# Windowed row maxima in blocks of 64 queries by 128 keys, on two column tiles of TensorE

## The reference

```python
# 1: attention with rotary positions, 16 heads of 16, over the last 64 keys
q, k = rotary(q), rotary(k)
attn = q @ k.T / 4
allowed = (j <= i) & (i - j < 64)
attn = softmax(where(allowed, attn, -inf)) @ v
x = layernorm(x + attn @ w_out.T)
# 2: a gated feed-forward with a shift by one token
x = layernorm(x + sigmoid(xr @ W_r.T) * (relu(xk @ W_k.T) ** 2 @ W_v.T))
# 3: linear attention with random features
x = layernorm(x + linear_attention(x, Wq, Wk, Wv, Wo, random_features))
# 4: a block with causal attention over all keys, and 8 experts of which each token takes 2
x = layernorm(x + block(x))
```

## Time and profile before

| | |
|---|---|
| median of 3 runs | 1870.25 us |
| the profiled execution's own time | 1865.49 us |
| its span, first to last instruction | 1863.7 us |
| TensorE, matmuls | 1708.6 us busy, 92% |
| TensorE, weight loads | 1100.9 us, 59% |
| VectorE | 1014.7 us, 54% |
| ScalarE | 887.6 us, 48% |
| GpSimd | 835.6 us, 45% |
| granted TensorE clock, mean | 0.959 |

### The profile page before, as it was taken

How to read it: one execution, slowest core, us unless ns; L and a number is a source line. 1 busy time by engine, 2 the same in 40 slices (tenths; PEclk the granted TensorE clock), 3 DMA queues, 4 the chain that set the end, 5 groups by cost and what they waited for, 6 DMA issues and landing times. The chain is left out here.

```text
span 1863.7 us, 32872 instructions
## 1 busy us (share of the span) xinstructions
PE 1708.6 (92%) x10796; PEld 1100.9 (59%) x10796; DVE 1014.7 (54%) x2357; ACT 887.6 (48%) x1877; POOL 835.6 (45%) x1295
## 2 busy tenths in 40 slices
PE   6888998999999999999999999999569999999992
PEld 4556766565567666556666654644337766667771
DVE  4547776877757786865788677886401100011014
ACT  2445454556665465675637467577322222212223
POOL 4664565432358683235858323446352211221123
PEclk9889998999999899999989999999779999999996
DMA  6655235042154404215432214050053133332126
GB/s 214 88 184 68 35 81 70 2 59 78 20 81 76 97 8 69 69 27 73 88 49 36 36 47 69 13 105 5 29 189 85 33 71 83 91 88 63 20 23 192
DMA packets 105668, 131.21 MB, mean 70 GB/s; under 512 B 15499, under 2 KB 77084, under 8 KB 105361
## 3 DMA queue, kind: packets, MB, share of 16 engines
q1 hardware_dynamic: 89104, 117.08, 29.3%
q0 software_dynamic: 14336, 11.41, 4.3%
q10 hardware_dynamic: 2064, 0.61, 0.2%
HBM read 53.96 MB, written 38.01 MB: 49 GB/s over the span
## 5 line engine op out<-in xcount | busy, mean ns | idle before, releaser
L1095 ACT ACTIVATE b_probs<-b_psum 128x512 f32<-128x512 f32 (+3 forms) x896 | 418.2, 547 | 190.3 <-PE b_psum L959 188.6
L1359 DVE TENSOR_REDUCE b_mneg<-b_psum 128x2 f32<-128x384 f32 (+5 forms) x608 | 333.2, 591 | 94.6 <-PE b_psum L946 92.4
L1458 POOL TENSOR_SCALAR_AFFINE_SELECT b_probs<-b_probs 128x512 f32<-128x512 f32 (+1 forms) x400 | 239.4, 610 | 292.9 <-ACT b_probs L1095 282.2
L946 PE MATMUL b_psum<-b_qk 96*128 96x192 bf16 (+4 forms) x1280 | 297.9, 299 | 4.2 <-DVE b_write_at L1319 1.2
L959 PE MATMUL b_psum<-b_qk 99*128 99x192 bf16 (+5 forms) x1344 | 262.9, 290 | 14.9 <-DMA b_qk<-b_mrow 11.2
L1689 POOL DMA_INDIRECT before_last_norm<-b_ye,b_ids x64 | 99.0, 1547 | 349.0 <-DMA before_last_norm<-b_ye,b_ids 191.5
L1784 ACT ACTIVATE b_hid<-b_psum,b_b 128x512 f32<-128x512 f32 (+1 forms) x136 | 90.0, 662 | 336.3 <-PE b_psum L1727 336.3
L1828 DVE TENSOR_TENSOR b_ye<-b_psum,b_b2b 128x512 f32<-128x512 f32 (+1 forms) x33 | 22.3, 675 | 388.9 <-PE b_psum L1735 388.9
L1735 PE MATMUL b_psum<-b_w,b_hid 128*128 128x256 f32 x1024 | 222.8, 379 | 0.6 <-ACT b_hid L1784 0.6
L1727 PE MATMUL b_psum<-b_xgt,b_w 128*128 128x512 f32 (+1 forms) x544 | 221.7, 567 | 0.0
L1735 PEld LDWEIGHTS b_psum<-b_w,b_hid 128*128 128x128 f32 x1024 | 193.9, 190 | 27.0 <-ACT b_hid L1784 1.0
(11 more groups left out here) (217 smaller groups left out, 2427.3 us busy)
## 6 DMA issues: line engine op xcount, KB each, us to landing
b_qk<-b_split SPq DMA_DIRECT2D x372, 128.0 KB, 5.1
b_w<-in_W SPq DMA_DIRECT2D x16, 1024.0 KB, 8.3
slot_rows<-before_last_norm SPq DMA_DIRECT2D x8, 1024.0 KB, 11.1
b_xg<-slot_rows SPq DMA_DIRECT2D x16, 512.0 KB, 9.6
before_last_norm<-b_early SPq DMA_DIRECT2D x4, 1024.0 KB, 4.9
b_o<-before_last_norm SPq DMA_DIRECT2D x4, 1024.0 KB, 5.7
before_last_norm<-b_o SPq DMA_DIRECT2D x4, 1024.0 KB, 4.4
b_rows<-before_last_norm SPq DMA_DIRECT2D x8, 512.0 KB, 7.4
```

What stands on the lines that cost most here:

```text
L946: ins = pe.matmul(out[:, i, :], q[0:KS, h, P * t:P * t + P], q[0:KS, HG + h, a:e], start=not last, stop=True, skip_group_check=True)
L1095: act.activation(probs_of((g, h2, t), a, e)[:, heads[0]:heads[-1] + 1, :], bank, ACT.Exp, scale=SCALE).then_inc(s.exp_done, 1)
L1359: dve.tensor_reduce(out, in_bank(("max",) + x[1:], heads, e - a), AX.X, ALU.max, negate=True).then_inc(s.max_read, 1)
L1458: ins = pool.affine_select(out=block, in_=block, pattern=[[0, HG], [1 if ahead else -1, z - y]], compare_op=ALU.is_ge, fill=none, base=y - ...
```

## The change

The windowed tile's keys are given as its own 128 (`key_spans`), and all its four heads go into one bank of 512 columns. Each tile of 128 queries is cut in two blocks of 64 queries. A block needs the 64 keys before it and its own 64, so 128 keys: the first block's scores go to partitions 0 to 63 of the bank, the second block's to partitions 64 to 127, each by a matmul with 64 stationary columns on its own half of the array (`tile_position`). One mask of 128 columns serves all tiles and is repeated for the four heads; a second one, for the first tile, hides the missing keys. A windowed group then has eight pieces, each with one mask matmul of 512 columns, eight score matmuls and one reduction of 512 columns.

`pieces` no longer asks whether a group is windowed. In the second pass, cells of 128 and of 64 queries therefore become one piece of four heads in place of two pieces of two. The estimated cost of `max` at L379 is not edited; it follows from the new numbers of heads and keys.

```diff
     def key_spans(self, g, t):
         if self.windowed[g]:
-            return [(max(0, P * t - WINDOW), P * t + P)]
+            return [(P * t, P * t + P)]
 ...
     def pieces(self, g, a, e):
-        n = 2 if self.windowed[g] else 4 if e - a <= P else 2 if e - a <= 2 * P else 1
+        n = 4 if e - a <= P else 2 if e - a <= 2 * P else 1
         return [(tuple(range(k, k + n)), a, e) for k in range(0, HG, n)]
 ...
                     if windowed[g]:
-                        pe.matmul(out, u.id16[:, :], u.mask_q[:, :, WQ - (e - a):WQ], start=True, stop=True,
-                                  skip_group_check=True)
-                    elif last:
+                        pe.matmul(out, u.id16[:, :], u.mask_q[:, int(t == 0), :].unsqueeze(1).broadcast_to([P, len(heads), P]),
+                                  start=True, stop=True, skip_group_check=True)
+                        for i, h in enumerate(heads):
+                            for y in range(2):
+                                at = P * t + WINDOW * y
+                                lo = max(0, at - WINDOW)
+                                ins = pe.matmul(out[WINDOW * y:WINDOW * y + WINDOW, i, lo - at + WINDOW:P],
+                                                q[0:KS, h, at:at + WINDOW], q[0:KS, HG + h, lo:at + WINDOW],
+                                                start=False, stop=True, tile_position=(0, WINDOW * y), skip_group_check=True)
+                        ins.then_inc(s.max_ready, 1)
+                        continue
+                    if last:
 ...
-    behind = p + WINDOW - w
-    mask_q = np.where((behind >= 0) & (behind < WINDOW), 0.0, NEG)
+    behind = p % WINDOW + WINDOW - f
+    near = (behind >= 0) & (behind < WINDOW)
+    mask_q, mask_first = np.where(near, 0.0, NEG), np.where(near & ((p >= WINDOW) | (f >= WINDOW)), 0.0, NEG)
 ...
-            [np.eye(P), mask_q, mask_q, np.where(f <= p, 0.0, NEG),
+            [np.eye(P), mask_q, mask_first, np.where(f <= p, 0.0, NEG),
 ...
-    sbuf(nc, ctx, u, "mask_q", [P, 2, WQ], BF16)
+    sbuf(nc, ctx, u, "mask_q", [P, 2, P], BF16)
 ...
-    width = [P, 2 * WQ, P, P]
+    width = [P, 2 * P, P, P]
```

More of the change, by code:

```diff
@@ L1502, in by_tile @@
         return np.tile(x.reshape(NT, P, HD).transpose(1, 0, 2), HG).astype(np.float32)
-    p, w, f = np.arange(P)[:, None], np.arange(WQ)[None], np.arange(P)[None]
-    behind = p + WINDOW - w
-    mask_q = np.where((behind >= 0) & (behind < WINDOW), 0.0, NEG)
+    p, f = np.arange(P)[:, None], np.arange(P)[None]
+    behind = p % WINDOW + WINDOW - f
+    near = (behind >= 0) & (behind < WINDOW)
+    mask_q, mask_first = np.where(near, 0.0, NEG), np.where(near & ((p >= WINDOW) | (f >= WINDOW)), 0.0, NEG)
     return {
```

## The result

The changed kernel takes 1877.28 us (median of six runs, 1874.61 to 1878.69); the kernel before, beside it, 1869.28 (1864.43 to 1870.53). The ratio is 1.005 with a 95% interval of 1.0037 to 1.0063: 8 us slower, where +5 was forecast and 1875 predicted. The profiled execution took 1877.8 us against 1865.5, so 12 us more, and what is read from the two traces concerns those 12. The size came out right. The experiments show that it is made of other terms than the sum had.

What follows compares the result with a forecast made beforehand. TensorE was taken to bound batches 1 to 3, batch 0 being latencies and loads. TensorE's tiles +6.4, relief -1.3 and batch 0 at 0 gave +5 us on the median of 1870.25: 1875 us, range 1860 to 1896.

Steps and rivals of the forecast that it cites:

- TensorE bounds batches 1 to 3: After 120 us TensorE, 96% busy, sets the pace; work added or removed there goes into the time one for one.
- the halved stream is given back: At seven of eight tiles, 0.22 us of streaming saved, 0.25 spent on two width changes and the exposed load.
- The sum of a tile: TensorE's cost of a windowed tile's maxima: 0.70 us, +0.04 at seven of eight tiles, +0.25 at tile 0.
- the weight load of a 64-column tile: Score matmuls: taken at the slow rate, 0.055 us, shown once ahead of the first pair; pairs at 0.058.
- rival B: Score matmuls: loads or streams of the two 64-column tiles don't overlap, +0.23 a tile, +22 us, 1897; chance 0.13.
- Relief of VectorE and ScalarE, -1.3: After 120 us: VectorE 49 us and ScalarE 9 us lighter; TensorE regains half of its 2.6 us of waits.
- Batch 0: Before 120 us, latencies and loads: between -5 and +3, taken as 0; the 8.4 us DMA wait isn't shortened.
- The order: Planner's static lists change with the maxima's estimated cost; idle time may move some 10 us either way; no term.
- rival C: The new order is bad, planned cost off by 0.26 a tile: 5 to 12 us of new waits, 1880 to 1887; chance 0.13.
- I expect none: TensorE's clock in the bursts: no fall expected, since streaming stays 0.44 of 0.70 us; no term.
- No drain (D): Width changes on TensorE cost nothing: 0.19 less a tile, -18 us on 96 tiles, 1857; chance 0.04.
- much relief (A): Lighter VectorE and ScalarE, fewer banks and batch 0 win more than the printed waits: -6 us, 1864; chance 0.20.

Runs made afterwards that it cites:

- e1: The changed kernel, order untouched, with the mask put in by two column-tiled matmuls of 64 stationary and 512 moving columns: 1854.87 us.
- e9 to e11: The changed kernel with the mask in column tiles too, planner told 0.55, 0.66 and 0.75 us for a windowed tile's maxima: 1856.3, 1848.88 and 1857.07 us.
- e4: The kernel before with only the second pass changed, cells of 128 and 64 queries as one piece of four heads: 1861.2 us.
- e3: The kernel before, work untouched, with the planner told 0.2195 us for each of a windowed tile's two pieces: 1859.76 us.

## Why the prediction was right, and what in it was not

- **TensorE bounds batches 1 to 3, and the halved stream is given back.** Right, and shown: the two changes of width are there with 0.095 us each, a tile costs 0.65 to 0.67 against 0.66, and taking 103 to 137 of some 550 changes away (e1, e9 to e11) brings 15.5 us at the same told cost, some of which may be the clock's.
- **The sum of a tile was 0.04 too high.** The mis-sized term is the weight load of a 64-column tile. I took the slow rate, 0.055 exposed and pairs 0.058 apart, 0.229 in all to the last pair's start behind the change of width; it was 0.19. So the load is nearer the fast end of my bounds. With 0.66 at every tile the term is 84 x 0 + 12 x (0.66 - 0.45) = +2.5 us in place of +6.4. (At tile 0 four of the eight matmuls have 64 columns, not one; their partners have 128, so the term stands. And the sixteen values matmuls would take 2.2 us one after another, not 2.1.)
- **Pairs overlap (rival B).** They do; B is out.
- **Relief of VectorE and ScalarE, -1.3.** The waits that I counted did not shrink together: those on maxima are gone in batch 1's burst and longer in batch 2's. TensorE's idle time in batch 1's stretch fell by 6 us, mostly in waits that I had not counted, by relief or by the list. The relief itself was 38 us of VectorE and 4 of ScalarE's exponentials, not 49 and 9: I multiplied mean durations, which overlap, where the busy time in the earlier trace rows has 111.5 + 12.7 = 124.2 us for the windowed reductions, and 108.4 - 21.9 = 86.5 is left of them. e4 leaves room for more, but can't be told from the list.
- **Batch 0, "nothing in the change shortens" the wait on the DMA, between -5 and +3.** The step that failed. The wait grew from 6.9 to 11.9 us, since the new list has SyncE issue six large DMAs while the rows come ready, and the instructions there came 13 us late. I read the wait in the earlier trace rows and did not look at what SyncE issued ahead of that DMA.
- **The order, "no term, but in the range", by some 10 either way.** The size was right, the place was not: it is the largest term of all. The reason I gave for rival C, that the planner is told too little, is not borne out as a rule: e3 is faster with the wrong cost. The changed work is fastest when told its true 0.66, but the mask in tiles, whose tile takes 0.46 in a run, is fastest at 0.66 as well. Rival C's mechanism, waits that weren't there, happened in part: the DMA, and two waits of 2.3 and 1.9 us on maxima in batch 2's burst.
- **"I expect none", a fall of the clock in the bursts.** Wrong for two of the three: 0.97 against 0.99 in batch 1's (120 to 300 us) and 0.96 against 0.99 in batch 2's (500 to 620), though 1.00 against 0.98 in batch 3's. With the 0.78 against 0.86 before 120 us the clock is a term that the sum put at nothing, and no run prices it by itself.
- **No drain (D), much relief (A).** D is out as said, and A too, since batch 1 was reached 13 us late and not 4 early. As forecast, the expert stage is unchanged: the 12.2 us at 1040 us are the 12.3 at the end. The forecast of 1875 against 1877 is luck in its sum: TensorE's term was 4 us too large, and the order, the DMA and the clock, left out or put at 0, can each be worth more than the 5 us of the whole sum.
- **The chances** gave slower 0.46, same 0.32 and faster 0.22. As measured, slower is right. For the work apart from its list, +4.9 with a standard error of 5.7, it is open which of the three is.

## What to carry to other kernels

Column tiles pay where a whole stretch of work stays at their width; a full-width matmul between tiled ones costs a change each way, here 0.095 us against some 0.2 that the tiles save. Put the mask into tiles too, and the same idea that lost brings 11 us over the work of before, from mean to mean and from best list to best list. And where a planner writes the order, run each version under three or four told costs before judging it: one list against one list here gave anything from -10 to +18 for the same edit. Behind a wait on a small DMA, look at when its data were ready, and at what its queue was given just before.

## What the runs showed of the hardware that I had not expected

- A 64-column bf16 tile loads faster than the float32 rate of the earlier trace rows: 0.055 us was expected to show ahead of the first pair. The 0.31 from mask to first pair leave nothing for it beside 0.22 and 0.095, and the three steps between pairs take 0.19 where their streams are 0.17, so 0.02 to 0.03 shows.
- Two matmuls with 64 stationary and 512 moving columns run side by side at full pace: 224.70 to 224.92, 0.22 us for both.
- A DMA of 12 rows behind six of 1 MB on one queue let TensorE wait 11.9 us: it was issued 7.2 us after its rows were ready, and TensorE went on 9.4 us after that. With the large ones moved, no DMA of this kind was waited for longer than 2.8 us before 130 us.
- Issuing a 1 MB DMA took SyncE 0.6 us for the first of the six and about 3 for the last three.
- With equal lists, four times of four, the kernel with 103 to 137 changes of width fewer had the higher granted clock, by 0.005 to 0.008.
